# First attention with the exponential between two copies and the values projected first, and the long convolution with exchanged operands

## What is computed

```python
x = _layernorm(x + _L0_attn_ref(x, ...))      # 32 heads, D_QK 32, 16 virtual keys, SCALE sqrt(32)
```

```python
Kf = jnp.fft.rfft(K, n=n, axis=-1)
xf = jnp.fft.rfft(x, n=n, axis=1)
y = jnp.fft.irfft(xf * Kf.T[None], n=n, axis=1)[:, :L]
...
y = y * (1.0 + mod_gate * scale_out) + mod_gate * shift_out
xt = x_text + y
h = layernorm(xt, g_ffn, b_ffn)
h = jax.nn.gelu(h @ W1 + b1, approximate=False) @ W2 + b2
return layernorm(xt + h, g_norm_out, b_norm_out)
```

## Time and profile before

| | us |
|---|---|
| median of 3 runs | 4504.68 (4503.95 to 4505.66) |
| profiled execution | 4501.69, of it span 4499.9 |
| main loop of the first attention, first to last mask matmul | 88.7 to 806.7 |
| convolution, first transfer to the next sublayer | 3085.89 to 3174.57 |
| end of the sublayer | 3174.57 to 3311.8 |

### The profile page before, as it was taken

How to read it: one execution, slowest core, us unless ns; L and a number is a source line. 1 busy time by engine, 2 the same in 40 slices (tenths; PEclk the granted TensorE clock), 3 DMA queues, 4 the chain that set the end, 5 groups by cost and what they waited for, 6 DMA issues and landing times. The chain is left out here.

```text
span 4499.9 us, 84989 instructions
## 1 busy us (share of the span) xinstructions
PE 3835.1 (85%) x33634; PEld 2573.7 (57%) x33634; DVE 2671.2 (59%) x7185; ACT 2146.1 (48%) x3795; POOL 1089.5 (24%) x754
## 2 busy tenths in 40 slices
PE   2888888787999789898999996555679998698999
PEld 2666666565666556664555553434457776465665
DVE  6677777565888557666656555982332222476555
ACT  2666666444555235555555444530554443454332
POOL 4444434222222211004454542221200000110000
PEclk8999999998999669999999997776789999798999
DMA  4222222000000010000000000004200000000000
GB/s 120 45 48 49 49 48 47 4 1 1 1 1 1 1 53 2 1 1 1 2 2 2 2 2 1 22 22 145 87 1 1 1 1 1 29 2 2 1 10 10
DMA packets 60472, 92.10 MB, mean 20 GB/s; under 512 B 16827, under 2 KB 43662, under 8 KB 58830
## 3 DMA queue, kind: packets, MB, share of 16 engines
q1 hardware_dynamic: 55948, 80.96, 7.7%
q10 hardware_dynamic: 4130, 5.72, 0.4%
HBM read 42.46 MB, written 10.62 MB: 12 GB/s over the span
## 5 line engine op out<-in xcount | busy, mean ns | idle before, releaser
L854 PE MATMUL banks<-XT,weight_region 128*128 128x512 f32 x1696 | 781.7, 599 | 1.4 <-DVE T L1229 1.4
L876 PEld LDWEIGHTS banks<-weight_region,HT 128*128 128x128 f32 x4672 | 560.8, 192 | 129.3 <-issue 107.4
L876 PE MATMUL banks<-weight_region,HT 128*128 128x128 f32 x4672 | 566.1, 275 | 7.1 <-ACT HT L1011 6.5
L1252 DVE SCALAR_TENSOR_TENSOR x_res<-banks,WT,x_res 128x128 f32<-128x128 f32 x800 | 225.0, 344 | 476.4 <-PE banks L876 437.4
L854 PEld LDWEIGHTS banks<-XT,weight_region 128*128 128x128 f32 x1696 | 305.8, 193 | 288.1 <-issue 285.3
L1006 ACT ACTIVATE HT<-banks,weight_region 128x512 f32<-128x512 f32 x256 | 173.3, 687 | 240.2 <-PE banks L854 234.0
L1069 POOL TENSOR_TENSOR FNM<-FNM,FRS 128x8 f32<-128x8 f32 x16 | 3.2, 202 | 1008.3 <-ACT FRS L965 1008.3
L458 DVE TENSOR_REDUCE MX<-banks 128x8 f32<-128x1152 f32 x128 | 173.2, 1353 | 116.6 <-PE banks L275 114.8
L384 ACT COPY PT<-banks 128x384 f32<-128x384 f32 x384 | 171.6, 481 | 134.1 <-PE banks L285 132.4
L1643 ACT COPY PT<-banks 77x512 f32<-77x512 f32 x256 | 143.0, 582 | 184.4 <-PE banks L1565 184.4
L1022 ACT ACTIVATE T<-banks 128x512 f32<-128x512 f32 x128 | 76.1, 597 | 233.9 <-PE banks L854 226.0
(11 more groups left out here) (488 smaller groups left out, 8529.7 us busy)
## 6 DMA issues: line engine op xcount, KB each, us to landing
FL<-RAW SPq DMA_DIRECT2D x512, 64.0 KB, 2.3
T<-s4d_k_dram SPq DMA_DIRECT2D x8, 1024.0 KB, 5.8
weight_region<-in_l_ffn__w_dram SPq DMA_DIRECT2D x2, 2048.0 KB, 7.6
film_dram<-F SPq DMA_DIRECT2D x8, 512.0 KB, 2.9
weight_region<-in_l_ffn__w_dram ACTq DMA_DIRECT2D x2, 2048.0 KB
FO<-film_dram SPq DMA_DIRECT2D x8, 512.0 KB, 4.1
x_res<-in_x_dram SPq DMA_DIRECT2D x1, 2048.0 KB
weight_region<-in_l_ffn__w_dram SPq DMA_DIRECT2D x2, 1024.0 KB, 9.7
```

Of the source, the lines that this page charges most:

```text
L854: nc.tensor.matmul(PS[:, q % 4, :], w, xt, start=True, stop=True).then_inc(s.h_ps, 1)
L876: ins = nc.tensor.matmul(PS[:, 4 + u % 2, b * P:(b + 1) * P], HT[:, u % 2, j, b * P:(b + 1) * P], w2[j], start=j == 0, stop=j == len(w2) - 1)
L1252: ins = nc.vector.scalar_tensor_tensor(R[:, t, :], PS[:, 4 + u % 2, b * P:(b + 1) * P], WT[:, t, e:e + 1], R[:, t, :], ALU.mult, ALU.add)
```

## The change

In `l0_attn` each iteration on PE now begins with T0 and T1 of step n-2, then `scores(n)`, then T2, then the due items, then the mix. The ring of two banks follows that order. On ACT the exponential of step n-1 stands between the copy of T1 and the copy of T2, and the items are read out after T2. The large subtraction on DVE is cut in two halves with a semaphore each (`sub_a` for banks 0 and 1, `sub` for banks 2 and 3); the first two mask matmuls wait for the first, the other two for the second. In `TAKE`, V now stands ahead of Q1.

In `s4d_conv` the operands are exchanged: the 32 columns of UR are stationary and the Toeplitz matrix moves. Four features write four strips of 32 partitions of a bank; ACT copies the bank to YT, PE transposes it back, and DVE writes it into `E.y_all`, a part of the weight region, so that nothing is stored to DRAM. U comes in four pieces, T has three buffers, and only the weights of the next sublayer are loaded here, on SP behind the Toeplitz matrices. Those of the experts are loaded in `l2_close`, and those of the third layer in `l2_ffn`.

```diff
-    TAKE = [["X"], ["K0", "Q0"], ["K1"], ["Q1", "V"], ["K2"], ["Q2"], ["K3"], ["Q3"]]
+    TAKE = [["X"], ["K0", "Q0"], ["K1"], ["V", "Q1"], ["K2"], ["Q2"], ["K3"], ["Q3"]]
...
                     if n >= 1:
-                        pe.wait_ge(s.sub, n)
+                        pe.wait_ge(s.sub_a, n)
...
                     for i in range(4):
+                        if i == 2 and n >= 1:
+                            pe.wait_ge(s.sub, n)
                         nc.tensor.matmul(PS[:, i, 0:2 * K], IDB[:], MASK[:].rearrange("p a k -> p (a k)"), start=True, stop=False)
...
                 for n in range(N + NR + 1):
+                    live = 2 <= n < N + 2
+                    if live:
+                        weights_T(n - 2, 0)
+                        weights_T(n - 2, 1)
                     if n < N:
                         scores(n)
...
-                    live = 2 <= n < N + 2
                     if live:
-                        weights_T(n - 2, 0)
-                        weights_T(n - 2, 1)
+                        weights_T(n - 2, 2)
                     for item, p in due(n):
                         produce(item, p)
                     if live:
-                        weights_T(n - 2, 2)
                         mix(n - 2, 0)
...
                         weights(3 * (n - 2) + 1)
+                    if 1 <= n <= N:
+                        act.wait_ge(s.sub, n)
+                        nc.scalar.activation(SM[:, (n - 1) % 3], SM[:, (n - 1) % 3], ACT.Exp, scale=SCALE).then_inc(s.ex, 1)
+                    if live:
+                        weights(3 * (n - 2) + 2)
                     for item, p in due(n):
                         take(item, p)
-                    if live:
-                        weights(3 * (n - 2) + 2)
-                    if n < N:
-                        act.wait_ge(s.sub, n + 1)
-                        nc.scalar.activation(SM[:, n % 3], SM[:, n % 3], ACT.Exp, scale=SCALE).then_inc(s.ex, 1)
...
-                    nc.vector.tensor_tensor(SM[:, n % 3, 1:9, :].rearrange("p (a i) k -> p i a k", a=2), sc[:, :, :, 0:P],
-                                            bc(MX[:, n % 2].unsqueeze(3), [P, 4, 2, P]), ALU.subtract).then_inc(s.sub, 1)
+                    main = SM[:, n % 3, 1:9, :].rearrange("p (a i) k -> p i a k", a=2)
+                    for h, done in ((0, s.sub_a), (2, s.sub)):
+                        nc.vector.tensor_tensor(main[:, h:h + 2], sc[:, h:h + 2, :, 0:P], bc(MX[:, n % 2, h:h + 2].unsqueeze(3), [P, 2, 2, P]),
+                                                ALU.subtract).then_inc(done, 1)
...
+                def toeplitz(c):
+                    if c >= 3:
+                        sp.wait_ge(s.yt_ps, c - 2)
+                    src = k_dram[c * DCH:(c + 1) * DCH, :]
+                    sp.dma_start(T[:, c % 3], bass.AP(tensor=src.tensor, offset=src.offset + 1, ap=[[1, P], [2 * P, DCH], [1, P]])).then_inc(t_ld[c % 3], 16)
...
+                for q in range(NU):
+                    sp.dma_start(U[:, q * BU:(q + 1) * BU], u_dram[:, q * BU:(q + 1) * BU]).then_inc(u_ld[q], 16)
                 for c in range(NCH):
...
+                    toeplitz(c)
+                for dst, src in prefetch:
+                    sp.dma_start(dst, src).then_inc(s.w_ld, 16)
...
+                def back(c):
+                    pe.wait_ge(s.yt, c + 1)
+                    if c >= 4:
+                        pe.wait_ge(s.y, c - 3)
+                    pe_transpose4(nc, [YT[:, c % 2, q, :] for q in range(4)], y_bank(c), E.ident).then_inc(s.y_ps, 1)
...
+                    for q in range(4):
+                        for i in range(4):
+                            ins = nc.tensor.matmul(yt_bank(c)[32 * i:32 * (i + 1), q * P:(q + 1) * P], UR[:, :, c * DCH + 4 * q + i], T[:, c % 3, 4 * q + i, :],
+                                                   start=True, stop=True)
+                    ins.then_inc(s.yt_ps, 1)
+                    if c:
+                        back(c - 1)
+                back(NCH - 1)
...
-                        ins = nc.tensor.matmul(PS[:, c, i * B_ALL:(i + 1) * B_ALL], T[:, c % 2, i, :], UR[:, :, c * DCH + i], start=True, stop=True)
...
-                    sp.dma_start(Y[:, g % 3], of(y_dram, g)).then_inc(loads[g % 3], 16)
                     sp.dma_start(FO[:, g % 3], of(fo_dram, g)).then_inc(loads[g % 3], 16)
+                    for dst, src in prefetch[g::NG]:
+                        sp.dma_start(dst, src).then_inc(s.w_ld, 16)
...
-        s4d_conv(nc, E, k_dram, u_dram, y_dram, place(["l2_ffw", "l2_ffn", "l3_attn", "l3_xattn"], 0))
-        run("l2_ffw", l2_close, y_dram=y_dram, fo_dram=fo_dram)
-        run("l2_ffn", l2_ffn)
+        E.y_all = region[:, REGION - B_ALL * P:REGION].rearrange("p (b d) -> p b d", b=B_ALL)
+        close, experts = place(["l2_ffw"], 0), place(["l2_ffn"], FFW, REGION - B_ALL * P)
+        s4d_conv(nc, E, k_dram, u_dram, close)
+        run("l2_ffw", l2_close, fo_dram=fo_dram, prefetch=experts)
+        run("l2_ffn", l2_ffn, prefetch=place(["l3_attn", "l3_xattn"], REGION - B_ALL * P))
```

More of the change, by code:

```diff
@@ L185, in due @@
         return [(item, n // NPR + 1) for item in TAKE[n % NPR]] if n // NPR + 1 < NP else []
-    with sublayer(nc, "cst vkc one xt_ps xt kq_ps raw flip0 flip1 cosm sinm rot v_ps v s_ps mx sub ex pt_ps pt z_ps shuf lnz rz zt o_ps res" + LN) as (s, ctx):
+    with sublayer(nc, "cst vkc one xt_ps xt kq_ps raw flip0 flip1 cosm sinm rot v_ps v s_ps mx sub_a sub ex pt_ps pt z_ps shuf lnz rz zt o_ps res" + LN) as (s, ctx):
         sb = E.scratch(ctx)
@@ L2627, in s4d_conv, with flip_bank, yt_bank, y_bank @@
     NCH = P // DCH
-    with sublayer(nc, "u_ld t_ld0 t_ld1 ur_ps ur y_ps y y_st w_ld") as (s, ctx):
+    NU = 4
+    with sublayer(nc, "u0 u1 u2 u3 t0 t1 t2 ur_ps ur yt_ps yt y_ps y w_ld") as (s, ctx):
         sb = E.scratch(ctx)
-        U = sb("U", [P, B_ALL, P]); Y = sb("Y", [P, B_ALL, P]); T = sb("T", [P, 2, DCH, P]); UR = sb("UR", [P, B_ALL, P])
-        t_ld = [s.t_ld0, s.t_ld1]
+        U = sb("U", [P, B_ALL, P]); UR = sb("UR", [P, B_ALL, P]); T = sb("T", [P, 3, DCH, P]); YT = sb("YT", [P, 2, 4, P])
+        u_ld = (s.u0, s.u1, s.u2, s.u3)
+        t_ld = (s.t0, s.t1, s.t2)
+        BU = B_ALL // NU
+        def flip_bank(c):
+            return PS[:, c % 4, :]
+        def yt_bank(c):
+            return PS[:, c % 4, :]
+        def y_bank(c):
+            return PS[:, 4 + c % 4, :]
         with nc.Block() as block:
@@ new lines, in _ @@
+                for c in range(NCH):
+                    toeplitz(c)
+                for dst, src in prefetch:
+                    sp.dma_start(dst, src).then_inc(s.w_ld, 16)
+                sp.wait_ge(s.w_ld, 16 * len(prefetch))
+            @block.tensor
+            def _(pe):
+                def back(c):
[3 more added lines that the diff above has]
+                    pe_transpose4(nc, [YT[:, c % 2, q, :] for q in range(4)], y_bank(c), E.ident).then_inc(s.y_ps, 1)
+                for c in range(8):
+                    if c % 2 == 0:
+                        pe.wait_ge(u_ld[c // 2], 16)
+                    if c >= 4:
+                        pe.wait_ge(s.ur, c - 3)
+                    nc.tensor.matmul(flip_bank(c), E.flip, U[:, 4 * c:4 * c + 4, :].rearrange("p b d -> p (b d)"), start=True, stop=True).then_inc(s.ur_ps, 1)
+                pe.wait_ge(s.ur, 8)
+                for c in range(NCH):
+                    pe.wait_ge(t_ld[c % 3], 16 * (c // 3 + 1))
+                    if c >= 4:
+                        pe.wait_ge(s.yt, c - 3)
+                    for q in range(4):
[6 more added lines that the diff above has]
+                back(NCH - 1)
@@ L2646, in _ @@
             @block.scalar
             def _(act):
-                for dst, src in prefetch:
-                    act.dma_start(dst, src).then_inc(s.w_ld, 16)
-                act.wait_ge(s.w_ld, 16 * len(prefetch))
-            @block.tensor
-            def _(pe):
-                pe.wait_ge(s.u_ld, 16)
-                for c in range(8):
-                    nc.tensor.matmul(PS[:, c, :], E.flip, U[:, 4 * c:4 * c + 4, :].rearrange("p b d -> p (b d)"), start=True, stop=True).then_inc(s.ur_ps, 1)
-                pe.wait_ge(s.ur, 8)
@@ L2658, in _ @@
                 for c in range(NCH):
-                    pe.wait_ge(t_ld[c % 2], 16 * (c // 2 + 1))
-                    for i in range(DCH):
-                        ins = nc.tensor.matmul(PS[:, c, i * B_ALL:(i + 1) * B_ALL], T[:, c % 2, i, :], UR[:, :, c * DCH + i], start=True, stop=True)
-                    ins.then_inc(s.y_ps, 1)
+                    act.wait_ge(s.yt_ps, c + 1)
+                    if c >= 2:
+                        act.wait_ge(s.y_ps, c - 1)
+                    nc.scalar.copy(YT[:, c % 2].rearrange("p q j -> p (q j)"), yt_bank(c)).then_inc(s.yt, 1)
@@ L2780, in film_rest @@
                 def film_rest(g):
[L2781 removed]
+                    pool.wait_ge(loads[g % 3], 16 * (g // 3 + 1))
```

34 lines of the change are left out of this document (11 added, 23 removed).

## The result

The changed kernel takes 4401.49 us (median of 4 runs, 4400.47 to 4405.54) against 4505.17 (4, 4503.95 to 4506.46) of the kernel before: ratio 0.9772, 95% interval 0.976 to 0.9784. The forecast was 4390, with a range of 4360 to 4428. The profiled execution is the slowest of the four, 4405.54.

The account below looks back on a forecast made before the run. No attention engine is full, so waits matter; the convolution's matmuls run at half clock, its transfers half the time. 4504.7 - 66 (attention) - 49 (convolution and sublayer's end) = 4389.7 us; range 4360 to 4428.

Parts of the forecast that it names:

- Both waits around the item vanish: Attention, PE: waits of 1.07 us around the item fall away, leaving 4.13 of 5.20 per iteration with one item.
- The exponential is covered: Attention, ACT: exponential of some 1.2 us hides behind scores, T2 and item (2.6); uncovered it adds 1.2 per iteration.
- Halves: Attention, DVE: two half subtractions cost +0.08 us, but DVE's loop becomes 4.09 in place of 4.30.
- n = 3, V: Attention iteration n mod 8 = 3: DVE reads V late, T0 is 0.9 us late: 6.95 in place of 6.1.
- n = 6 and 7, `turn`: Attention: n = 6 waits for turn's transfers, 5.3 for 4.13; n = 7 has DVE's loop on the path, 5.5 for 5.1.
- n = 0 and 1 behind the scaling: Attention iterations n mod 8 = 0 and 1: walked at 4.5 and 5.1 us.
- The transfers are the pace: Convolution: Toeplitz transfers of 1.05 MB at 310 GB/s, taken as 3.5 us a chunk, 28.0 in all, set the pace.
- rival 1: Convolution: matmuls stay the bound at 0.214 us each, 11 us saved with FO, total 4428; chance 0.07.
- `l2_close`: Sublayer after the convolution: first work waits for FO alone, 4.1 us for 5.56, 1.4 more saved.
- Rival 2: Attention: ACT becomes the bound, up to 5.55 us an iteration, total 4450, in part 4412 to 4450; chance 0.12.
- Rivals 3 and 4: 3: ACT's chain exceeds 12.1 us per two attention iterations, 4514 and up, chance 0.03; 4: more waits vanish, chance 0.10.
- Rival 4: Attention waits vanish further, 4.85 us an iteration, with a full convolution gain: 4365, 4350 to 4368; chance 0.10.

Follow-up runs that it names:

- k_order: Changed kernel with undivided subtraction, exponential at the end of ACT's iteration and Q1 ahead of V, leaving PE's order and T2 ahead of items on ACT: 4423.24 us.
- e_explast: Changed kernel with the exponential of step n back at the end of ACT's iteration, PE's order unchanged: 4417.28 us, ratio 0.9811.
- d_whole: Changed kernel with the large subtraction in one piece and all masks waiting for it: 4420.95 us, ratio 0.9822.
- c_take: Changed kernel with Q1 again ahead of V in TAKE: 4397.27 us, ratio 0.9761.
- h_best: Changed kernel with Q1 ahead of V, third and fourth turn one iteration later, scaling at n = 3 mod 16, four T buffers: 4373.11 us.
- g_quiet4: Changed kernel with the layer norm's scaling moved from n = 7 to n = 2 mod 16, and four T buffers for three: 4383.01 us, ratio 0.9741.
- m_best2: Changed kernel with Q1 ahead of V, late turns, scaling at n = 3 mod 16, and DVE reading V ahead of spread: 4358.16 us.
- i_oldop: Changed kernel with the convolution's old operands (Toeplitz matrix stationary, 32 columns moving), its other edits kept: 4420.13 us, ratio 0.9822.

## Why the prediction was right, point by point

- **The sum.** The median came 11.8 above the forecast of 4389.7. The saving is 103.7 for 115, 11.3 short. The attention gave 61.5 for 66, the convolution with the sublayer's end 44.3 for 49. In the two profiled executions untouched sublayers lost 9.7 more, which I had not reckoned with; against the medians 7.5 of that goes away, and 2 stay.
- **Both waits around the item vanish.** Right: 4.13 to 4.19 with one item for 4.13, and the weight loads of line 300 wait for ACT 12.2 us (110 to 740) for 63.0 before (110 to 800). `k_order` shows that the order does this, without the rest.
- **The exponential is covered.** Right. Its price uncovered was wrong: not 1.2 an iteration, but 0.17 (`e_explast`), since PE felt it in half of the iterations only.
- **Halves.** Right, and shown by `d_whole`: the loop of DVE at 4.30 with one subtraction, hidden with two.
- **n = 3, V.** 7.17 for 6.95: right in kind, the edit costs 6 us (`c_take`).
- **n = 6 and 7, `turn`.** Here the walk failed. I charged the wait for the transfers to the interval n = 6 alone (5.3; it takes 4.81 or 5.06) and gave n = 7, with the projection and `turn`'s own 1.2, 5.5. It takes 6.05 to 7.3, as `turn` ends late and the maximum, both halves and the projection follow it in a row. `h_best` shows it: with the turn later, 5.03 to 5.39.
- **n = 0 and 1 behind the scaling.** I had left the layer norm out of the walk; 0.9, seven times, and `g_quiet4`, which moves it away from GpSimd, has it back. With n = 7 and n = 3 it made eight iterations 40.65 on the mean of fourteen groups ((655.1 - 54.1 - 31.9) / 14, without the first and the last group) where I had walked 40.1; n = 2, 4 and 6 came out shorter than walked and took part of it back. The 0.05 an iteration that I allowed "for what I don't see" covered it by luck.
- **The transfers are the pace.** Right in mechanism: bursts of 1.25 with waits for T between them. Mis-sized was the term 8 x 3.5: it is 8 x 3.61, at 290 GB/s for 310, and start, U and the last landing took 9.2 (the last burst starts 38.1 behind U's issue in `g_quiet4`, less 28.9) for 7.4. Of these 9.2, U takes 8.0 (its last quarter lands there), and the late fourth matrix 1.3 (4.9 for 3.6). In after the last burst starts 39.1 behind U's issue, for 35.4. Then the 5.5 of the tail was right for a last burst at half clock, as in after; at full clock the tail is 4.2.
- **Strided weights (rival 1).** Refuted: 32 instructions with weights at a stride of 512 bytes take 1.25 to 1.28 at full clock; the 1.4 at most that I had taken from the mix held. By the rule of the Trainium skill (TensorE: Matmul & The Clock Gate, Part 3, The mechanism) that I had weighed, loads and matmuls of one row group would be serial; the same section also lets a load go ahead into a background weight buffer, which I had left out. In after the 32 loads of a burst are shown busy for 1.06 of the 1.25 us of their matmuls, so they overlap in the records. Since the ends of matmuls are modelled there, how much they do is not settled; what is settled is that the price is that of the mix.
- **`l2_close`.** 0.3 saved for 1.4: DVE's first work came 4.92 after the start for the 4.1 that I took from the median landing; the expert weights share the engines with the first FO. Whether they cause it was not tried.
- **Rival 2, ACT as the bound.** Not seen in after, though `e_explast` is a part of it at 4417.
- **Rivals 3 and 4.** Nothing became slower. Rival 4, 4.85 an iteration, did not come with this change, but `h_best` (38.3 and 38.9 for eight, 4.79 and 4.86 each) and `m_best2` reach it with the small edits above.

## What to carry to other kernels

Where a ring of banks makes an engine wait, first put the item whose predecessor is read out early; only when these waits are gone do finer cuts of the other engines' loops pay, and then they pay together more than apart. (That they pay nothing before is concluded from DVE's loop of 4.30, hidden behind 5.20 before; no run has the finer cuts without the order.) After such a change look again for what came once in eight or sixteen iterations: here a late transfer, a bank that is read last and four small instructions beside GpSimd held 41 us (655 to 614) that the first pass left. Judge edits of a few us by the stage's own length, not by the median.

## What the hardware showed that I had not expected

**DVE and GpSimd.** A scaling of 128 elements a partition on DVE takes 0.34 alone and 1.31 beside GpSimd's products (above).

**The clock falls on a busy PE.** In `i_oldop` the old form went to 1.2 GHz with PE and PEld at 2.00 of 2.00 us; in the kernel before it ran there from end to end:

```profile
3111.80:3167.00 55.20, 54.79 (x256) 54.69 (x256) 5.12 (x8) 0.00 (x0) 0.00 (x0) 0.50 0.49 134
```

Why the clock falls there was not tried. The exchanged form makes the same product in fewer microseconds of PE, 1.25 for 3.4 a chunk at full clock and 2.05 for 6.8 at half, so its half-clock stretches lie under the transfers.

**Untouched sublayers differ by the clock they meet.** From the last mask to the convolution it is 2279.5 before, 2286.6 in after, 2272.6 in `g_quiet4`, and 2272.5 to 2289.3 over all runs, whatever was edited. Most of the 14.0 between after and `g_quiet4` is in the same two sublayers, with the same instructions (`l1_attn` and the cross attention behind it, first of after, then of `g_quiet4`):

```profile
1419.40:1574.40 155.00, 120.58 (x469) 86.79 (x469) 91.89 (x369) 36.76 (x76) 30.53 (x28) 0.67 0.02 7
1574.40:1813.80 239.40, 214.61 (x3028) 149.94 (x3027) 159.07 (x265) 123.73 (x199) 28.01 (x16) 0.91 0.06 22
```

```profile
1409.20:1559.70 150.50, 114.51 (x469) 81.28 (x469) 90.45 (x369) 36.62 (x76) 30.51 (x28) 0.73 0.02 8
1559.70:1793.70 234.00, 209.09 (x3028) 146.23 (x3027) 159.00 (x265) 123.57 (x199) 28.04 (x16) 0.94 0.06 22
```

155.0 for 150.5 at a granted clock of 0.67 for 0.73, and 239.4 for 234.0 at 0.91 for 0.94: 9.9 us. `c_take` and `h_best` have 239.4 again. What decides in which way a run goes stays open.
